# Storing both parts of each turned tile of tokens, and loading them straight into place

## The reference, cut to what matters

```python
def reference(x, Wq, Wv, Wg, Wo, beta, ln_g, ln_b, router_w, w1, v1, w2):
    xn = layernorm(x)                                  # 4096 tokens x 1024
    q, v = xn @ Wq, xn @ Wv
    state[t] = sigmoid(beta) * state[t-1] + v[t]       # per sequence
    y = layernorm(q * state) * ln_g + ln_b
    attn = (y * silu(xn @ Wg)) @ Wo
    # experts: the 8 of 64 with the largest softmax(xn @ router_w.T), each takes at most 128 tokens
    h = silu(xg @ w1[e].T) * (xg @ v1[e].T)            # F = 384
    ffn[tok] += weight * (h @ w2[e])
    return x + attn + ffn
```

## Time and profile before

| | |
|---|---|
| time, median of 3 runs | 2558.32 us (2557.31 to 2558.71) |
| the profiled execution: its time | 2558.36 us |
| its span, first to last instruction | 2556.7 us |
| PE busy (matmul) | 2501.3 us, 98% |
| DVE, ACT, POOL busy | 1630.1, 1319.9, 672.0 us |
| mean granted TensorE clock | 0.989 |
| DMA moved | 605.74 MB, mean 237 GB/s |
| stages on PE | block 0: 10.7 to 330.9 us; block 1: to 577.4; blocks 2 to 6: 326.3 each, to 2208.7; block 7 and the last expert: to 2556.7 |

### The profile page before, as it was taken

The page is one execution under the profiler, slowest core; times in us unless marked ns, Lnnn a source line. Parts: engine busy times, 40 slices in busy tenths (PEclk is TensorE's granted clock), DMA queues, the critical chain, the costliest instruction groups (busy, mean ns, idle before and its releaser), DMA issues.

```text
span 2556.7 us, 39295 instructions
## 1 busy us (share of the span) xinstructions
PE 2501.3 (98%) x13649; PEld 2221.5 (87%) x13649; DVE 1630.1 (64%) x1689; ACT 1319.9 (52%) x1499; POOL 672.0 (26%) x523
## 2 busy tenths in 40 slices
PE   7999999999999999999999999999999999999997
PEld 6887987898889988899888898888998889988897
DVE  6765797665666666566665666666665665666654
ACT  4555522464455644565454565445654456545554
POOL 2111122222232232322232222322232232322321
PEclk9998999999999999999999999999999999999999
DMA  7774765696667976669866698666986668866686
GB/s 268 251 276 163 230 203 195 204 297 231 229 214 235 303 246 227 210 206 322 259 217 212 202 309 280 191 226 208 288 284 202 222 227 279 270 229 224 197 271 172
DMA packets 151790, 605.74 MB, mean 237 GB/s; under 512 B 20592, under 2 KB 37040, under 8 KB 151216
## 3 DMA queue, kind: packets, MB, share of 16 engines
q1 hardware_dynamic: 116304, 518.91, 56.6%
q0 software_dynamic: 35424, 86.00, 16.1%
HBM read 520.89 MB, written 100.70 MB: 243 GB/s over the span
## 4 chain that ended last, share of the span: by engine, by line
PE 92%; DVE 3%; DMA 2%; ACT 2%; issue 1%; POOL 0%; SPq 0%; DVEq 0%; ACTq 0%; POOLq 0%
PE psA L1543 18%; PE psA L1545 18%; PE psA L1544 18%; PE psH L1543 7%; PE psH L1545 7%; PE psH L1544 7%; PE psY L1543 4%; PE psY L1545 3%; PE psY L1544 3%; PE psX L1650 2%; PE psY L1575 2%; PE psX L1670 1%; PE psH L1689 1%; DMA ew_raw<-ew_dram 1%; PE psY L1705 1%
## 5 line engine op out<-in xcount | busy, mean ns | idle before, releaser
L1156 DVE TENSOR_TENSOR ew_lo<-ew_raw,ew_hi 128x1536 fp32r<-128x1536 f32 x384 | 694.0, 1816 | 332.8 <-ACT ew_hi L752 318.4
L752 ACT ACTIVATE ew_hi<-ew_raw 128x1536 fp32r<-128x1536 f32 x384 | 568.3, 1484 | 157.4 <-DMA ew_raw<-ew_dram 122.3
L1543 PE MATMUL psA<-xT_hi,pw_hi 128*128 128x512 f32 (+1 forms) x1544 | 623.9, 404 | 3.3 <-DVE xT_lo L1073 2.6
L746 ACT ACTIVATE pw_hi<-pw_raw 128x1024 fp32r<-128x1024 f32 x254 | 266.3, 1059 | 675.3 <-PE psA L1545 673.5
L1545 PE MATMUL psA<-xT_hi,pw_lo 128*128 128x512 f32 (+1 forms) x1544 | 612.7, 397 | 0.0
L1544 PE MATMUL psA<-xT_lo,pw_hi 128*128 128x512 f32 (+1 forms) x1544 | 609.0, 394 | 0.0
L1151 DVE TENSOR_TENSOR pw_lo<-pw_raw,pw_hi 128x1024 fp32r<-128x1024 f32 x256 | 313.8, 1236 | 159.0 <-ACT pw_hi L746 153.7
L1543 PE MATMUL psH<-ew_hi,gT_hi 128*128 128x384 f32 x1024 | 352.9, 345 | 2.1 <-DVE ew_lo L1156 1.4
L1545 PEld LDWEIGHTS psA<-xT_hi,pw_lo 128*128 128x128 f32 x1544 | 294.0, 190 | 69.8
L1544 PEld LDWEIGHTS psA<-xT_lo,pw_hi 128*128 128x128 f32 x1544 | 296.7, 192 | 63.8
L1543 PEld LDWEIGHTS psA<-xT_hi,pw_hi 128*128 128x128 f32 x1544 | 293.2, 190 | 64.7 <-issue 4.4
(11 more groups left out here) (161 smaller groups left out, 3350.9 us busy)
## 6 DMA issues: line engine op xcount, KB each, us to landing
ew_raw<-ew_dram SPq DMA_DIRECT2D x384, 768.0 KB, 6.3
pw_raw<-proj_w_dram SPq DMA_DIRECT2D x256, 512.0 KB, 5.2
xn_scratch<-xt SPq DMA_DIRECT2D x33, 512.0 KB, 5.8
xt<-x_dram SPq DMA_DIRECT2D x32, 512.0 KB, 6.5
out_dram<-x_dram SPq DMA_DIRECT2D x32, 512.0 KB, 6.1
out_dram<-ot POOLq DMA_DIRECT2D x32, 512.0 KB, 12.5
xn<-xn_turned SPq DMA_DIRECT2D x29, 512.0 KB, 3.9
xn_turned<-xraw SPq DMA_DIRECT2D x28, 512.0 KB, 5.1
```

Source lines behind the costliest of these rows:

```text
L746: act.activation(dst[:, slot, :, :], pw_raw[:, slot, :, :], ACT.Copy).then_inc(s_pwhi, 1)
L752: act.activation(ew_hi[:, c % 3, :], ew_raw[:, c % 3, :], ACT.Copy).then_inc(s_ewhi, 1)
L1156: dve.tensor_tensor(ew_lo[:, c % 3, :], ew_raw[:, c % 3, :], ew_hi[:, c % 3, :].bitcast(F32), ALU.subtract).then_inc(s_ewlo, 1)
L1543: pe.matmul(dst, l_hi, r_hi_, start=first, stop=False)
```

## The change

- `xT_hi` and `xT_lo` are laid out tile by tile: [P, NT, KC, P] instead of [P, KC, 512]. A projection's moving operand of 512 columns is now `hi[:, :, k, :]`, four runs of 128 elements.
- In the router, ACT no longer makes the copy `xraw`; DVE's `low(k)` reads PSUM instead. SP stores `rt_hi` and `rt_lo` (two DMAs of 512 KB per tile instead of one) once `low` is done, and ACT waits for both before it writes that buffer again. ACT turns over tile k (`turned_hi(k)`) before it normalizes tile k+1, no longer after it. For the last eight tiles PE's `turn_tile(k)` waits for `low(k-1)` and not only for `turned_hi(k-1)`.
- Between blocks, `load_xT(j, mm)` loads both parts of a tile straight into `xT_hi` and `xT_lo` (two DMAs of 512 KB instead of one). `take_xT` and `xT_lo_of` (28 each) and the buffer `xn` are gone. In the SP order the pair stands after `load_rest` (blocks 2 to 6), after `load_first` (block 1), and after the two `pw_raw` loads (block 0). It waits for nothing but the block's last gate projection; PE waits for all eight DMAs (`s_xTl`) before the next block's first matmul.

The core of the diff:

```diff
-        xT_hi = place("xT_hi", [P, KC, TB], F32R)
-        xT_lo = place("xT_lo", [P, KC, TB], F32R)
+        xT_hi = place("xT_hi", [P, NT, KC, P], F32R)
+        xT_lo = place("xT_lo", [P, NT, KC, P], F32R)
@@ SP, router_step
-                    wait_alone(sp, s_praw, k - NT)
-                    sp.dma_start(turned[k - 1, :, :], xraw[:, (k - 1) % 2, :, :].rearrange("p k c -> p (k c)")
-                                 ).then_inc(s_tst[(k - 1) % 2], 16)
+                    wait_alone(sp, s_plo, k)
+                    for i, t in enumerate((rt_hi, rt_lo)):
+                        sp.dma_start(turned[k - 1, i, :, :], t[:, (k - 1) % 2, :, :].rearrange("p k c -> p (k c)").bitcast(F32)
+                                     ).then_inc(s_tst[(k - 1) % 2], 16)
@@ SP
+            def load_xT(j, mm):
+                for i, t in enumerate((xT_hi, xT_lo)):
+                    sp.dma_start(t[:, bass.ds(mm, 1), :, :].rearrange("p t k c -> p (t k c)").bitcast(F32),
+                                 turned[bass.ds((j + 1) * NT + mm, 1), i, :, :].rearrange("a p c -> p (a c)")
+                                 ).then_inc(s_xTl, 16)
@@ SP, block 0
-            load_xn(NT)
+            sp.wait_ge(s_pj, ng(0, KC - 1) + 1)
             for mm in range(KC // 2):
                 if mm == 1:
                     store_w(NB - 1)
-                next_xn(0, mm)
                 for w in range(2):
                     load_proj(0, 3 * KC + 2 * mm + w + 4)
+                load_xT(0, mm)
@@ SP, block 1
-                next_xn(1, mm)
                 if mm > 0:
                     load_rest(mm)
                 ...
                 else:
                     load_first(mm + 1)
+                if mm == 0:
+                    sp.wait_ge(s_pj, ng(1, KC - 1) + 1)
+                load_xT(1, mm)
@@ SP, blocks 2 to 6
+                    load_rest(e0 + 7 + mm)
                     if not last:
-                        next_xn(j, mm)
-                    load_rest(e0 + 7 + mm)
+                        sp.wait_ge(s_pj, ng(j, KC - 1) + 1)
+                        load_xT(j, mm)
@@ ACT
-                if k >= NT:
-                    if k >= NT + 2:
-                        wait_alone(act, s_tst[k % 2], 16 * ((k - NT) // 2))
-                    act.activation(xraw[:, k % 2, :, :], chunks(bank_of(k)), ACT.Copy).then_inc(s_praw, 1)
+                if k >= NT + 2:
+                    wait_alone(act, s_tst[k % 2], 16 * (k // 2 * 2 - NT))
@@ ACT, router_step
+                turned_hi(k)
                 if k + 1 < NTILE:
                     normalize(k + 1)
-                turned_hi(k)
@@ DVE, low
-                raw = chunks(bank_of(k)) if k < NT else xraw[:, k % 2, :, :]
-                dve.tensor_tensor(dst, raw, hi.bitcast(F32), ALU.subtract).then_inc(s_plo, 1)
+                dve.tensor_tensor(dst, chunks(bank_of(k)), hi.bitcast(F32), ALU.subtract).then_inc(s_plo, 1)
@@ PE, proj
-                    o = three(psA[:, bank, :], pw_hi[:, slot, k, :], pw_lo[:, slot, k, :], hi[:, k, :],
-                              lo[:, k, :], k == 0, k == KC - 1)
+                    o = three(psA[:, bank, :], pw_hi[:, slot, k, :], pw_lo[:, slot, k, :], hi[:, :, k, :],
+                              lo[:, :, k, :], k == 0, k == KC - 1)
@@ PE, run(j)
-                wait_alone(pe, s_xlo, 4 * j)
+                wait_alone(pe, s_xTl, 32 * NT * j)
```

More of the change, by code:

```diff
@@ L124, in build @@
         ln6T = place("ln6T", [P, KC, P], F32R)
-        xn = place("xn", [P, KC, P], F32)
-        at_o = top[0]
         ot = place("ot", [P, 2 * NT, 2 * P], F32)
-        xraw = place("xraw", [P, 2, KC, P], F32, at_o)
         at_e = top[0]
@@ L191, in build @@
         scratch = nc.dram_tensor("xn_scratch", (NTOK + P, XW), F32).ap()
-        turned = nc.dram_tensor("xn_turned", (NTOK // P + 1, P, D), F32).ap()
+        turned = nc.dram_tensor("xn_turned", (NTOK // P, 2, P, D), F32).ap()
         unused = nc.dram_tensor("unused", (2, P, 4), F32).ap()
@@ L253, in build @@
         s_acc = sem("s_acc")
-        s_xnl = sem("s_xnl")
-        s_xhi, s_xlo = sem("s_xhi"), sem("s_xlo")
+        s_xTl = sem("s_xTl")
         s_ew = [sem(f"s_ew{u}") for u in range(3)]
@@ L397, in load_piece @@
                 sp.dma_start(ew_raw[:, c % 3, :], ew[e, c, :, :]).then_inc(s_ew[c % 3], 16)
-            def load_xn(tile):
-                sp.dma_start(xn[:, :, :].rearrange("p k c -> p (k c)"),
-                             turned[bass.ds(tile, 1), :, :].rearrange("a p c -> p (a c)")).then_inc(s_xnl, 16)
+            def load_xT(j, mm):
[3 more added lines that the diff above has]
+                                 ).then_inc(s_xTl, 16)
             def load_rest(e, cs=range(3)):
@@ L411, in load_first @@
                     load_piece(e, c, PIECES * e - 2 + c)
-            def next_xn(j, mm):
-                sp.wait_ge(s_xlo, 4 * j + mm + 1)
-                load_xn((j + 1) * NT + mm + 1)
             for k in range(NT):
@@ L445, in _ @@
             router_step(NTILE)
-            sp.dma_start(turned[NTILE, :, :], xt[:, 7, :]).then_inc(s_spare, 16)
             sp.dma_start(scratch[NTOK:NTOK + P, 0:D], xt[:, 7, :]).then_inc(s_spare, 16)
@@ L451, in _ @@
             for u in range(2):
-                sp.wait_ge(s_tst[u], 16 * (NTILE - NT) // 2)
-            load_xn(NT)
+                sp.wait_ge(s_tst[u], 16 * (NTILE - NT))
+            sp.wait_ge(s_pj, ng(0, KC - 1) + 1)
             copied = NT
@@ L658, in _ @@
                         pool.wait_ge(s_xst[u], 16 * (NTILE // 8))
-                    pool.wait_ge(s_spare, 48)
+                    pool.wait_ge(s_spare, 32)
                     gather(0)
@@ L716, in turned_hi @@
                 act.wait_ge(s_pT, k + 1)
-                dst = xT_hi[:, :, k * P:(k + 1) * P] if k < NT else rt_hi[:, k % 2, :, :]
-                if k >= NT:
-                    if k >= NT + 2:
-                        wait_alone(act, s_tst[k % 2], 16 * ((k - NT) // 2))
-                    act.activation(xraw[:, k % 2, :, :], chunks(bank_of(k)), ACT.Copy).then_inc(s_praw, 1)
+                dst = xT_hi[:, k, :, :] if k < NT else rt_hi[:, k % 2, :, :]
+                if k >= NT + 2:
+                    wait_alone(act, s_tst[k % 2], 16 * (k // 2 * 2 - NT))
                 act.activation(dst, chunks(bank_of(k)), ACT.Copy).then_inc(s_phi, 1)
@@ L870, in out_weights @@
                             n2(0, 0, 1) + 1, out_room(mm)[0])
[L872 to L877, removed]
             for mm in range(KC // 2):
@@ L887, in _ @@
                     logits_lo(NB - 1)
-                take_xT(0, mm)
                 out_copy(0, mm, 0)
@@ L916, in _ @@
             for mm in range(2):
-                if mm == 0:
-                    take_xT(1, 0)
                 out_copy(1, mm, 0)
@@ L929, in _ @@
                     hT_hi_of(0)
-                    take_xT(1, 1)
                     piece_hi(1, 0)
@@ L944, in run_out @@
                 hT_hi_of(e)
-                if not last:
-                    take_xT(j, mm)
                 piece_hi(e + 1, 0)
@@ L1068, in low @@
                 dve.wait_ge(s_phi, k + 1)
-                c = slice(k * P, (k + 1) * P)
-                dst, hi = (xT_lo[:, :, c], xT_hi[:, :, c]) if k < NT else (rt_lo[:, k % 2, :, :],
+                dst, hi = (xT_lo[:, k, :, :], xT_hi[:, k, :, :]) if k < NT else (rt_lo[:, k % 2, :, :],
                                                                          rt_hi[:, k % 2, :, :])
-                raw = chunks(bank_of(k)) if k < NT else xraw[:, k % 2, :, :]
-                dve.tensor_tensor(dst, raw, hi.bitcast(F32), ALU.subtract).then_inc(s_plo, 1)
+                dve.tensor_tensor(dst, chunks(bank_of(k)), hi.bitcast(F32), ALU.subtract).then_inc(s_plo, 1)
             def take_logits(q):
@@ L1244, in starts @@
                 wait_alone(dve, s_st0, j + 1)
[L1246 to L1250, removed]
             def gain_rows():
@@ L1362, in _ @@
                     top8_of(NB - 1)
-                xT_lo_of(0, mm)
                 if mm == 0:
@@ L1429, in _ @@
             lo_z7(1)
-            xT_lo_of(1, 0)
             for w in range(2):
@@ L1438, in _ @@
             hT_lo_of(0)
-            xT_lo_of(1, 1)
             piece_lo(1, 0)
@@ L1449, in run_out @@
                 hT_lo_of(e)
-                if not last:
-                    xT_lo_of(j, mm)
                 piece_lo(e + 1, 0)
@@ L1552, in turn_tile @@
                 if k >= NTILE - KC:
-                    pe.wait_ge(s_phi, k)
-                    pe.wait_ge(s_plo, k - 1)
+                    pe.wait_ge(s_plo, k)
                 elif k >= NT:
@@ L1573, in logits @@
                     for i in range(2):
-                        t = (xT_hi, xT_lo)[i][:, c, k * P:(k + 1) * P] if k < NT else (rt_hi, rt_lo)[i][:, k % 2, c, :]
+                        t = (xT_hi, xT_lo)[i][:, k, c, :] if k < NT else (rt_hi, rt_lo)[i][:, k % 2, c, :]
                         o = pe.matmul(psY[:, q % 2, s * 2 * SEL:(s + 1) * 2 * SEL], t, r_hl[:, c, :],
```

(6 more changed lines are left out.)

3 lines of the change are left out of this document (1 added, 2 removed).

## The result

The changed kernel takes 2645.1 us (median of 4 runs, 2639.58 to 2652.32) against 2558.52 us for the kernel before (4 runs, 2557.31 to 2560.06): ratio 1.034, 95% interval 1.0314 to 1.0365. It is slower, as predicted, but by 87 us and not by 40: 2645 lies outside the range of 2572 to 2624. The profiled execution took 2645.55 us, its span is 2643.8 us, the mean granted clock 0.985.

What follows compares the result with a forecast made beforehand. PE, busy 98% of the span, bounds the kernel; relieving ACT and DVE wins only PE's waits and low clock, in block 0. 2558.4 - 21 + 57 + 3.7 = 2598 us, range 2572 to 2624.

Steps and rivals of the forecast that it cites:

- Part 1: Router in block 0: shorter PE waits (-7.5 us) and less low clock (-13.5), a gain of 21 us.
- Part 2: Transfers between blocks: PE waits for late-landing pairs at block ends, plus low clock behind the waits, a loss of 57 us.
- The clock: Low clock behind PE's waits at the ends of blocks 1 to 6: 7 us taken each, costing 3.5 us.
- Rival D: Output stages bound by the DMA engines, pairs some 4 us later, block 0 worse too: 2626 us, chance 0.18.
- Part 3: V, Q and gate projections: moving operand in four runs costs 3.7 us over 4608 matmuls, bounds 0 and 11.
- The excess: Output projection, 256 columns in two runs: 122.7 ns measured against 121.9 for one run, so 0.8 ns.
- once per matmul: V, Q and gate projections: the 0.8 ns is paid once for each of 4608 matmuls, 3.7 us.
- A line through 384 and 512 columns: From 177.5 and 233.1 ns, 256 columns in one run of the output projection should take 121.9 ns.
- The upper bound of 11 us: V, Q and gate projections: most the four runs could cost, with the 0.8 ns paid for three breaks.

Runs made afterwards that it cites:

- e5: e4 with the old layout of xT_hi and xT_lo, each load writing 512-byte runs: 2541.5 us, ratio 0.9942 to the kernel before.
- e7: e4 with ACT's old order, normalize of tile k+1 ahead of turned_hi(k): 2592.21 us, ratio 1.0133 to the kernel before.
- e12: e4, but in blocks 2 to 6 only the last of a stage's four pairs goes ahead of the weight pieces: 2587.05 us, ratio 1.011.
- e4: The changed kernel with the pair of xT loads ahead of the weight pieces in blocks 1 to 6: 2574.07 us, ratio 1.0065 to the kernel before.
- e1: The kernel before with only the new tile-by-tile layout of xT_hi and xT_lo, four runs of 128: 2590.87 us, ratio 1.0127.
- e3: The kernel before with the output projection's 256-column moving operand in one run instead of two: 2553.02 us, ratio 0.998.
- e2: The kernel before with each projection's moving operand read as two runs of 256 columns (values wrong): 2574.11 us, ratio 1.0059.
- e11: The kernel before with each projection's moving operand read as eight runs of 64 columns (values wrong): 2632.06 us, ratio 1.0294.
- e6: e5 with the 512-byte runs on the store side in block 0 and loads by chunks: 2546.45 us, ratio 0.9961 to the kernel before.

## Why the direction was right and the size was not

**Part 1, block 0: right.** Predicted -21; measured -17.2 with the new layout in it, and 313.41 - 3.01 - 330.86 = -20.5 in e5, which has the same ACT and DVE work and the old layout. The five waits on `rt_lo` went, the waits on `xt` in block 0 are 5.3 us (4.8 predicted: 3.4 - 2.0 + 3.4), 17.1 us of low clock stayed (14 predicted). That the order of two ACT instructions carries the larger part, e7 showed: 11 of the 20.

**Part 2, the transfers: right in place, kind and nearly in size.** The mechanism (pair behind three weight pieces, second half landing some 10 us after the pair's issue) is what the trace shows: 15.5 us for a predicted 14.9 at the end of block 1, and 4.8 to 5.6 for a predicted 4.1 at the five others. Of the excess, 0.6 to 0.7 us a wait is the time from landing to PE's first matmul, which the prediction put at nothing. The clock was over-priced: 1.6 to 3.0 us at each block end for a predicted 3.5, because 0.2 to 3.2 us of each low stretch (12.1 at the end of block 1) lay in the wait itself, where it costs nothing, and one stretch was only 3.4 us long. That waits and clock together came out at 56.0 us for a predicted 56.9 is luck: the two errors, +6.9 and -7.8, nearly cancel. What was missing is that four pairs per stage push the weight pieces back: 10.9 us in the output stages (e12). Rival D had the right sign here (a full queue lengthens everything), but took it as pairs that land 4 us later still, which did not happen; and the DMA engines are no bound, since e4 moves the same bytes without a wait behind block 0. The Trainium skill ("DMA: Bandwidth & Descriptors", section Bandwidth) has 6.15 us for 1 MB on free DMA engines. In this case's full queue `xT_lo`, 512 KB, took 9.8 us at the median, and in e4 8.9.

**Part 3, the moving operand in four runs: the step that failed.** "The excess is 0.8 ns ... 3.7 us if it is once per matmul, which I take; the bounds are 0 and three breaks, 11 us." It is 7.0 or 13.3 ns a matmul: 33 us alone (e1), 36 us in the stages after. This one term is 32 of the 48 us that the prediction lacked. It failed three times over. A line through 384 and 512 columns, drawn on to 256, gave the unbroken price of the broken row, and was itself 1.1 ns too high (e3: 1.9 ns and not 0.8). The excess of a break at 256 columns was taken for one at 512, where e2 shows 3.4 ns by the run times. And "once per matmul" was chosen against "per break" with no row for it; e2, e1 and e11 show that it grows with their number. The upper bound of 11 us was built from the same 0.8 ns, so it bounded nothing.

The Trainium skill ("SBUF — State Buffer", section Door 1) has full rate for consecutive accesses within 16 bytes; by it, runs of 512 bytes are free. The measurement decides: e1 costs 33 us with 512-byte runs, e2 16 us with 1 KB runs. The rule may hold for the read of a line and says nothing of what a new run costs; what that is in PE, no run here shows.

## What to carry to other kernels

When an edit changes only the address pattern of the matmul that fills the kernel, measure a group of that very matmul in both patterns, since 7 ns times 4608 is 32 us, twice the longest single wait here (15.5); an extrapolated fraction of a nanosecond is no price, and no bound either. Keep the matmul's operand in one run and let the DMA have the short runs: in e5 that gave 33 us, and behind block 0 nobody waited for the loads. Put a transfer where its queue has a gap, ahead of the one that will block on a semaphore: the same bytes cost 71 us more in one place than in the other.

## What was not expected of the hardware

- A matmul of 512 columns (float32 in the matmul type) costs more with each break in its moving operand: 3.4, 7.1 and 16.3 ns for one, three and seven breaks by the run times, on some 233 ns. Between one and seven only the number of breaks differs. Groups of 48 don't spread but fall on steps: 11.19 (no break), 11.2 or 11.51 (one), 11.52 or 11.83 (three), 12.08 us (seven). What picks the step is open.
- In a busy queue, runs of 512 bytes cost a transfer of 512 KB about a microsecond or less. Stores that wrote them into DRAM took 6.0 and 7.3 us against 5.2 and 6.1 (e6 and e5). For loads that wrote them into SBUF the last semaphore update in the trace came after 9.5 us against 8.9 (e5 and e4).
- Behind waits of 4.8 to 5.6 us PE was busy for only 3.2 to 6.1 us at 1.2 GHz.
